# Metaformer block on one core: low parts of the first four tiles made early, QK units by token block, input over two queues

## What is computed

```python
x = x + conv(ln_c(x))                  # attention block
#   ln_c(v) = (v - mean) / sqrt(var + 1e-6), over the 384 channels
#   qkv = ln_c(x) @ w_qkv + b_qkv;  12 heads of 32 channels
#   attn = softmax(q * scale @ k.T + rel_h + rel_w);  out = attn @ v @ w_proj + b_proj
t = t + moe(ln_t(t))                   # router, top 2 of 8 experts, capacity, 384 -> 1536 -> 384
```

## Time and profile before

| | us |
|---|---|
| median of 3 runs | 599.11 (598.87 to 599.52) |
| profiled execution | 598.25, its span 596.4 |
| TensorE busy | 582.9 (98%) |
| VectorE busy | 378.0 (63%) |
| ScalarE busy | 294.4 (49%) |
| GpSimd busy | 216.0 (36%) |

### The profile page before, as it was taken

The page is one execution under the profiler, slowest core; times in us unless marked ns, Lnnn a source line. Parts: engine busy times, 40 slices in busy tenths (PEclk is TensorE's granted clock), DMA queues, the critical chain, the costliest instruction groups (busy, mean ns, idle before and its releaser), DMA issues.

```text
span 596.4 us, 11424 instructions
## 1 busy us (share of the span) xinstructions
PE 582.9 (98%) x4441; PEld 506.4 (85%) x4441; DVE 378.0 (63%) x630; ACT 294.4 (49%) x409; POOL 216.0 (36%) x133
## 2 busy tenths in 40 slices
PE   7999999999999999999989999999999999999996
PEld 7787977766677766767978999999999999999994
DVE  6646777676787766713998855554577455367523
ACT  4555245455555545563665444444645444455524
POOL 1400068889898888898640000000000000000002
PEclk9999999999999999999999999999999999999999
DMA  7146064444333344103323444444433434443302
GB/s 228 60 88 135 1 133 89 90 90 82 67 65 68 71 88 88 41 2 108 129 70 115 140 144 158 160 160 145 131 122 122 146 131 160 158 159 95 105 1 106
DMA packets 38615, 63.40 MB, mean 106 GB/s; under 512 B 3912, under 2 KB 34478, under 8 KB 38446
## 3 DMA queue, kind: packets, MB, share of 16 engines
q1 hardware_dynamic: 38574, 62.83, 37.1%
HBM read 44.16 MB, written 1.57 MB: 77 GB/s over the span
## 4 chain that ended last, share of the span: by engine, by line
PE 88%; DVE 4%; DMA 2%; ACT 1%; SPq 1%; POOL 1%; issue 1%; POOLq 0%; DVEq 0%
PE ps L886 21%; PE ps L902 21%; PE ps L659 13%; PE ps L668 9%; PE ps L563 8%; PE ps L646 7%; PE ps L595 2%; PE ps L913 1%; DMA xs<-in_x 1%; PE ps L606 1%; SPq L378 1%; PE ps L692 1%; DMA kst<-kp 1%; DVE tl L1373 1%; POOL dsp L502 1%
## 5 line engine op out<-in xcount | busy, mean ns | idle before, releaser
L1275 DVE TENSOR_REDUCE rhalf<-ps 128x1 f32<-128x512 f32 x192 | 130.9, 690 | 33.0 <-PE ps L646 32.7
L467 POOL TENSOR_TENSOR acc<-acc,prob 128x1024 f32<-128x1024 f32 x58 | 139.7, 2409 | 8.7 <-ACT prob L1060 4.0
L1060 ACT ACTIVATE prob<-ps 128x1024 f32<-128x1024 f32 x96 | 98.1, 1028 | 80.1 <-PE ps L659 80.0
L659 PE MATMUL ps<-qst,kst 128*128 128x512 f32 x384 | 115.3, 396 | 0.5 <-DMA qst<-mneg 0.3
L886 PE MATMUL ps<-xeh,wih 128*128 128x320 f32 x288 | 89.6, 311 | 1.0 <-ACT xeh L1122 1.0
L510 POOL CAST dpc<-dpt 120x1024 fp32r<-120x1024 f32 (+1 forms) x3 | 3.1, 1041 | 240.6 <-PE ps L922 216.5
L902 PE MATMUL ps<-hh,woh 128*128 128x320 f32 x288 | 89.2, 310 | 0.0
L902 PE MATMUL ps<-hh,wol 128*128 128x320 f32 x288 | 89.0, 309 | 0.0
L886 PE MATMUL ps<-xeh,wil 128*128 128x320 f32 x288 | 89.0, 309 | 0.0
L902 PE MATMUL ps<-hl,woh 128*128 128x320 f32 x288 | 89.0, 309 | 0.0
L886 PE MATMUL ps<-xel,wih 128*128 128x320 f32 x288 | 89.0, 309 | 0.0
(11 more groups left out here) (169 smaller groups left out, 885.9 us busy)
## 6 DMA issues: line engine op xcount, KB each, us to landing
raw_i<-in_L_ffn_wi SPq DMA_DIRECT2D x32, 576.0 KB, 5.1
raw_o<-in_L_ffn_wo SPq DMA_DIRECT2D x32, 576.0 KB, 4.1
xs<-in_x SPq DMA_DIRECT2D x8, 384.0 KB, 4.5
qst<-qh SPq DMA_DIRECT2D x12, 256.0 KB, 3.1
qst<-relh SPq DMA_DIRECT2D x12, 256.0 KB, 3.9
qst<-relw SPq DMA_DIRECT2D x12, 256.0 KB, 4.4
kst<-kp SPq DMA_DIRECT2D x12, 256.0 KB, 5.1
qst<-ql SPq DMA_DIRECT2D x12, 128.0 KB, 3.0
```

The lines of the kernel that those rows point to most:

```text
L467: nc.gpsimd.tensor_tensor(acc[:, :], acc[:, :], prob[:, slot_of(j, t), :], ALU.add).then_inc(sum_add, 1)
L659: last = mm(bank(2 * (t % 2) + half), kst[b][:, part, t * P:(t + 1) * P], qst[b][:, part, half * BANK:(half + 1) * BANK], start=part == 0, ...
L1060: run(prob[:, slot_of(j, t), :], ps[:, 2 * (t % 2) * BANK:2 * (t % 2 + 1) * BANK], ACT.Exp).then_inc(exp_done, 1)
L1275: ve.tensor_reduce(rhalf[:, p // 2, p % 2:p % 2 + 1], bank(max_bank(b, p)), AX_X, ALU.max).then_inc(max_red, 1)
```

## The change

Five edits, all in the head of the program.

1. `xnl` is laid out as half, chunk, token. The low part of the first half then fills just the space of tiles 0 to 3 of `xs`.
2. VectorE makes the three low parts of the first half inside the second half's norm, behind the variance step and ahead of the reciprocal and of the products that normalise tiles 4 to 7 (`behind`). The low parts of the second half come behind the small copies of the tables and behind one low part of the weights, which stands earlier than it did.
3. QK units of chunk 0 are ordered by half: q and k of the first half, then q and k of the second (before: both halves of q, then both of k). The banks are 7, 6, 4, 5 instead of 7, 4, 5, 6, since 4 and 5 hold transposed input until the second half's low parts are made.
4. TensorE runs the first QK unit, and then transposes the second half.
5. SyncE issues the transfers of tiles 0 to 3 only; ScalarE, as its first instructions, those of tiles 4 to 7. The identity follows the second transfer on SyncE as before.

```diff
-    xnh, xnl = place("xnh", [P, DC, T], F32R, u2), place("xnl", [P, DC, T], F32R, x0)
+    xnh, xnl = place("xnh", [P, DC, T], F32R, u2), place("xnl", [P, 2, DC, BANK], F32R, x0)
...
-        QK = [(kk, c, half) for c in range(DC) for kk in range(2) for half in range(2)]
-        QK_BANKS = [7, 4, 5, 6]
+        QK = [(kk, 0, half) for half in range(2) for kk in range(2)]
+        QK += [(kk, c, half) for c in range(1, DC) for kk in range(2) for half in range(2)]
+        QK_BANKS = [7, 6, 4, 5]
...
-            for n in range(NT // XT):
+            for n in range(NT // XT // 2):
                 sp.dma_start(xs[:, n * XT:(n + 1) * XT, :], x_v[:, n * XT:(n + 1) * XT, :]).then_inc(x_in[n], 16)
-                if n == 1:
-                    sp.dma_start(ident[:, :], ident_c).then_inc(ident_in, 16)
+            sp.dma_start(ident[:, :], ident_c).then_inc(ident_in, 16)
...
-                if half == 0:
+                if n < 2:
+                    pe.wait_ge(w_lo, n + 1)
+                elif n % 2 == 0:
                     pe.wait_ge(w_lo, n // 2 + 1)
-                if n < 2:
-                    pe.wait_ge(turn_dve, DC * (n + 1))
+                if n in (0, 2):
+                    pe.wait_ge(turn_dve, DC * (half + 1))
...
-                if n == 3:
+                if n == 1:
                     pe.wait_ge(bd_ready, 2)
...
-            for n in range(4):
+            qk(0)
+            turn_x(1)
+            for n in range(1, 4):
                 qk(n)
...
+            for n in range(NT // XT // 2, NT // XT):
+                act.dma_start(xs[:, n * XT:(n + 1) * XT, :], x_v[:, n * XT:(n + 1) * XT, :]).then_inc(x_in[n], 16)
             norm(xs, xn, 0)
...
                 ve.tensor_scalar(veps[:, 0:HALF], mv[:, n % 2 * HALF:(n % 2 + 1) * HALF, 1], eps, None, ALU.add).then_inc(ln_var, 1)
+                behind()
                 dve.wait_ge(ln_std, n + 1)
...
+            def lows_back(half):
+
+                for c in range(DC):
+                    dve.wait_ge(turn_act, DC * half + c + 1)
+                    ve.tensor_tensor(xnl[:, half, c, :], bank(X_TURNS[DC * half + c]),
+                                     xnh[:, c, half * BANK:(half + 1) * BANK].bitcast(F32), ALU.subtract).then_inc(turn_dve, 1)
...
-            turn_back(xnl, xnh, 0, X_TURNS[0:DC])
-            turn_back(xnl, xnh, 0, X_TURNS[DC:2 * DC], DC)
+            def first_half_back():
+
+                dve.wait_ge(xn_dve, HALF // 2)
+                dve.wait_ge(xn_act, HALF // 2)
+                lows_back(0)
...
+            norm(xs, xn, LN_C_EPS, 0, x_ready)
+            norm(xs, xn, LN_C_EPS, 1, x_ready, behind=first_half_back)
...
+            dve.wait_ge(w_lo, 1)
+            weights_low(1)
+            dve.wait_ge(xn_dve, NT // 2)
+            dve.wait_ge(xn_act, NT // 2)
+            lows_back(1)
```

More of the change, by code:

```diff
@@ L547, in turn, with turn_x @@
                     last.then_inc(turned, 1)
-            for half in range(2):
+            def turn_x(half):
                 pe.wait_ge(xn_dve, HALF // 2 * (half + 1))
                 pe.wait_ge(xn_act, HALF // 2 * (half + 1))
-                if half == 0:
-                    pe.wait_ge(ident_in, 16)
                 turn(xn, X_TURNS[DC * half:DC * (half + 1)])
-                if half == 0:
-                    turn_tables()
-                    keep_warm(3)
+            pe.wait_ge(ident_in, 16)
+            turn_x(0)
+            turn_tables()
+            keep_warm(3)
             def three(out_bank, stationary, moving, first=True, last=True):
@@ L582, in qk @@
                     last = three(bank(QK_BANKS[n % 4]), [w[:, c, m * P:(m + 1) * P] for w in (wqkh, wqkl)],
-                                 [x_[:, c, half * BANK:(half + 1) * BANK] for x_ in (xnh, xnl)], c == 0, c == DC - 1)
+                                 [xnh[:, c, half * BANK:(half + 1) * BANK], xnl[:, half, c, :]], c == 0, c == DC - 1)
                 last.then_inc(proj_mm, 1)
@@ L628, in value_tile @@
                 for c in range(DC):
-                    last = three(bank(V_BANKS[t % 4], D), [x_[:, c, t * P:(t + 1) * P] for x_ in (xnh, xnl)],
+                    last = three(bank(V_BANKS[t % 4], D), [xnh[:, c, t * P:(t + 1) * P], xnl[:, t // HALF, c, t % HALF * P:(t % HALF + 1) * P]],
                                  [w[:, c, :] for w in (wvh, wvl)], c == 0, c == DC - 1)
@@ L1196, in ln_next, with norm @@
                 ins.then_inc(ln_step, count)
-            def norm(src, dst, eps, n, ready, order=range(HALF)):
+            def norm(src, dst, eps, n, ready, order=range(HALF), behind=lambda: None):
                 tiles = range(n % 2 * HALF, (n % 2 + 1) * HALF)
@@ L1232, in _, with x_ready @@
             ve.memset(bd[:, :, :, :], 0.0).then_inc(bd_zero, 1)
[L1233 to L1236, removed]
-            turn_back(xnl, xnh, 0, X_TURNS[0:DC])
-            turn_back(xnl, xnh, 0, X_TURNS[DC:2 * DC], DC)
+            def first_half_back():
+                dve.wait_ge(xn_dve, HALF // 2)
+                dve.wait_ge(xn_act, HALF // 2)
+                lows_back(0)
+            def x_ready(t):
+                dve.wait_ge(x_in[t // XT], 16)
+            norm(xs, xn, LN_C_EPS, 0, x_ready)
+            norm(xs, xn, LN_C_EPS, 1, x_ready, behind=first_half_back)
             dve.wait_ge(bd_zero, 1)
@@ L1250, in units @@
                     cols = slice(half * BANK, (half + 1) * BANK)
-                    if half == 0:
-                        if n == 0:
-                            dve.wait_ge(w_lo, 1)
+                    if n > 0 and n % 2 == 0:
                         weights_low(n // 2 + 1)
```

## The result

| | before | after |
|---|---|---|
| median, us | 598.65 (22 runs, 597.46 to 599.91) | 600.02 (22 runs, 598.90 to 601.85) |
| ratio | | 1.0025, 95% interval 1.0014 to 1.0035 |
| profiled execution, us | 598.25 | 601.02 |
| its span | 596.4 | 599.2 |
| mean granted clock | 1.000 | 0.994 |

I had forecast 599.0 from a median of 599.11, no change that can be told. The median lies inside my range, but the move of 1.4 us is real, and I had given it 22 in 100.

What follows compares the result with a forecast made beforehand. TensorE, 88% of the chain, was taken as the bound, so only its head could shift. Relative products at L + 17.8 = 24.1 us (L = 6.3) against 24.24 gave 599.1 - 0.1 = 599.0 us, range 598.0 to 600.1.

Steps and rivals of the forecast that it cites:

- The thread from L to the first matmul: Head: first half's norm, second half's statistics, three low parts in sequence; first QK matmul at L + 7.7 us.
- L: Time when the second input transfer (tiles 2 and 3) has landed: 4.93 us before, taken as 6.3 after.
- q: Start time of QK unit 0, the first QK matmul, put at L + 7.7 us.
- The QK stage with transposes inside: From first QK matmul to relative products: 8.36 us of units, 1.53 of transposes, 0.2 for changes of matmul kind.
- Equal sharing: Input over two queues: all four transfers share the DMA engines equally and end together at 7.1 us.
- my yardstick: Old head's timeline: second transfer landed at 4.93 us, relative products at 24.24; a shift there should reach the end unchanged.
- The clock: TensorE falling to its slower rate after idling in the head; 1 to 2 us, counted only within rival C.
- rival C: Input: lagging DMA engine hits the first half, L 8.7, head 2.3 us later, 601.4 us or more; chance 0.22.
- the vanished wait: Head: VectorE's 1.06 us wait before the second half's statistics (8.00 to 9.06) goes with two queues.
- A shift that does not arrive: Behind the head: a shift at 24.24 us not reaching the end, named as another way of being wrong; no size.
- B: Input: first half not delayed, L under 5.2, gain 0.6 to 1.5 us, put at 597.7 us; chance 0.17.
- D: QK stage: unit 1 or 2 waits on VectorE, costing 0.3 to 0.8 us, 599.3 to 599.8; chance 0.05.

Runs made afterwards that it cites:

- e6: The change with SyncE issuing tiles 0-1 and 4-5, ScalarE tiles 2-3 and 6-7; 597.64 us, ratio 0.9981 to the kernel before.
- e4: The change itself timed again, nothing altered; 598.69 us, ratio 0.9996 to the kernel before.
- e2: The change with all four input transfers issued by SyncE, new order kept; 597.04 us, ratio 0.9980 to the kernel before.
- e10: The change itself timed a third time, nothing altered; 598.99 us, ratio 1.0011 to the kernel before.
- e12: Repeat of e7 on another chip; 596.63 us, ratio 0.9964 to the kernel before.
- e5: The change with ScalarE waiting for the first input transfer to land before issuing tiles 4 to 7; 599.51 us, ratio 1.0008 to the kernel before.
- e9: The kernel before with 12 instead of 3 warming matmuls between the two halves' transposes; 597.55 us, ratio 0.9983.
- e7: e2 with 7 instead of 3 warming matmuls behind the tables; 596.29 us, ratio 0.9963 to the kernel before.
- e1: The change with 35 instead of 22 warming matmuls before the transposes and 10 instead of 3 behind the tables; 598.59 us, ratio 1.0001 to the kernel before.
- e11: The change with 34 instead of 22 warming matmuls before the transposes and 8 instead of 3 behind the tables; 598.15 us, ratio 0.9993 to the kernel before.
- e3: The kernel before with only the input split over two queues, old order kept; 599.80 us, ratio 1.0022.
- e8: The change with 12 instead of 22 warming matmuls before the first transposes; 600.95 us, ratio 1.0041 to the kernel before.

## Why the prediction was wrong, point by point

*The thread from L to the first matmul: right.* q = L + 7.7 gives 14.57 for L = 6.87; measured 14.56. In e6, with the statistics running through from 4.85, it gave 13.6; measured 13.56. The match to 0.01 is luck: in the profile of the change the second statistics, up to the variance step, took 0.2 us less than summed and a pause of 0.26 us ahead of the low parts made up for it, and e4, with 14.18 - 6.67, shows 7.5. To 0.2 us the durations of a head that is one thread can be added.

*The QK stage with transposes inside: right, 0.3 too dear.* 9.80 and 9.82 us (e2, e4) against 10.09.

*L: direction right, size off.* I took 6.3 and measured 6.7 to 6.9 in the profiles of the change (after, e4, e10). The step that failed was to pull towards the lower end because of an expected bubble and a late start of ScalarE's queue: ScalarE issued at 0.72 us, as early as SyncE. Equal sharing was the right reading. I had also overpriced a transfer: 384 KB at the 392 GB/s of the earlier trace rows are 1.00 us, not 1.09, and with that equal sharing gives 3.84 + 3.0 = 6.85, not 7.1; measured 6.84. Worth 0.4 to 0.6 us. The 4.93 of my yardstick was early, too: in the four other profiles with one queue tiles 2 and 3 came at 5.2 to 5.7.

*The clock: the step that failed, a term that the sum put at nothing.* I priced it only within rival C, for an idle stretch of 4 us. My sum has L in it, and with L the idle stretch ahead of the transposes: L + 3.73 - 8.2 is 1.8 us at L = 6.3 and 2.4 at 6.87, in a head that already had one of 1.86. I took 1.86 without a fall in one profile as a proof of safety. A single execution cannot give that: e4 keeps the clock over 1.98, e12 loses it behind 1.95, e5 behind 2.12, e10 behind 2.54. In the first measurement 11 of 22 executions of the change stand above 600.4 (not 10, as I wrote ahead of e10) and 11 below 599.7, and ten of the upper eleven have a mean clock of 0.996 or less. The fall costs 2.1 us here and 1.3 in the kernel before.

*The baseline: an assumption of one execution.* I treated the profiled execution of before as typical. It had the clock, and it also had the lagging DMA engine, 1.06 us of waiting. In e9, which has the same single queue, the third transfer landed at 6.7, not 9.0, and VectorE did not wait. The gain of 1.06 us that I booked for the vanished wait exists only in the executions that have the lag; how many have it is not known. The kernel before with its clock kept is at 598.07.

*A shift that does not arrive: the second term that the sum lacked, named only as what would prove me wrong.* Behind the head the change loses 0.6 us more than before at the third head's gather. Where the head was as forecast (e4: relative products at 24.00, my 24.1), the span was still 0.5 us over that of before, 596.9 against 596.4, which is the head's -0.24 and the rest's +0.74.

*Rivals.* B did not happen: SyncE's second transfer is delayed, to 6.7 us or later, in every two-queue profile that starts both queues together. C is refuted in its cause: the lag does not belong to a time. In no profile with the queues in parallel does the last of an input transfer's sixteen shares land more than 0.3 us behind the last but one, while with the single queue the worst such lag was 0.4 to 2.4 us in each of its five profiles. What I had hung onto C, the slow clock, came without it. D was seen once (e7), at 0.5 us.

*The sum again.* From the profile of before to that of after: +0.4 for L against its break-even, -0.3 for the cheaper QK stage, +2.0 for the clock, +0.7 behind the head; together 2.8, measured 601.02 - 598.25 = 2.77. Over the medians it is 1.4, since the kernel before has the slow clock in some of its executions too. The clock is not the whole of the miss: the change's lower groups, at 598.7 to 599.1, are 0.6 to 1.0 above the 598.07 of the kernel before with its clock kept, where I had forecast 0.1 less. The lower group of the first measurement, 599.1, is 0.4 above the 598.7 of e4 and e10; there is no profile of it, and that stays open, as do the few executions of e1, e9 and e11 that stand 1 to 2.3 us above the others with a full clock. What decides whether a stretch of some 2 us costs the clock is open as well.

## What to carry to other kernels

In this kernel a second issuing queue brought the later data earlier at the cost of the first, so put what is needed first on both queues (e6) or leave the order to one (e2). When a step makes TensorE wait longer, price its clock as a term of its own with a chance, and fill the stretch with warming matmuls before judging a reordering. When one profile stands for a kernel whose runs spread by 2 us, ask which of its groups that execution belongs to.

## What the runs showed of the hardware

- Two queues with work shared the DMA engines in pieces well under a transfer: 384 KB on each landed at 4.8 and 5.2 us, where one alone landed at 3.8.
- The granted clock fell to its lower level behind idle stretches of 1.70 (e3), 1.95 (e12), 2.12 (e5), 2.48 and 2.54 us (after, e10), and held over 1.86 (before), 1.98 (e4) and 2.31 (e3); behind 4.69 us (e8) it fell, and the mean clock was low in all eleven executions. With more warming matmuls no execution of e1, e7, e9 and e11 had a mean clock under 0.998, and one in six of e12.
- The same 44 records of warming matmuls ended at 7.5 to 8.7 us, because TensorE's rate rose from 7 to 11 or 12 a microsecond at a different moment in each execution (5:6 us: 7 in e4, 11 in e10).
- With one long queue the last share of an input transfer lagged by 0.4 to 2.4 us (five profiles), with two shorter ones by 0.3 us at most (eight profiles).
- An instruction fetch of 16 KB took 1.0 to 1.4 us of one DMA engine. In the eight profiles where it fell among the third head's gathers TensorE waited 0.3 to 0.9 us for one; in the six others it did not wait. That the one causes the other is not shown.
